# Routed experts: results scattered to (choice, token) rows, and read back by plain loads

## What is computed

```python
logits = xt @ Wr + br
probs = jax.nn.softmax(logits, axis=-1)
top_p, top_idx = jax.lax.top_k(probs, 2)            # two choices per token
weights = top_p / top_p.sum(axis=-1, keepdims=True)
h = gelu(xe @ W1 + b1)                              # per expert; hidden 256 in L0, 1024 in L1
y = h @ W2 + b2
out = (weights[:, :, None] * sel).sum(axis=1)       # sel: the two chosen experts' rows of y
x = x + out
```

## Time and profile before

| | us |
|---|---|
| median of 3 runs (5113.29 to 5120.27) | 5113.97 |
| the profiled execution, its own time | 5105.49 |
| span of that execution | 5103.5 |
| mean granted TensorE clock, share of full | 0.919 |
| L0: from the last `y` to the next phase's first instruction | 95.2 |
| L1: from the last `y` to the next phase's first instruction | 95.1 |

### The profile page before, as it was taken

The page is one execution under the profiler, slowest core; times in us unless marked ns, Lnnn a source line. Parts: engine busy times, 40 slices in busy tenths (PEclk is TensorE's granted clock), DMA queues, the critical chain, the costliest instruction groups (busy, mean ns, idle before and its releaser), DMA issues. The chain is left out here.

```text
span 5103.5 us, 70265 instructions
## 1 busy us (share of the span) xinstructions
PE 4142.4 (81%) x21605; PEld 3192.0 (63%) x21605; DVE 2765.3 (54%) x5823; ACT 1344.4 (26%) x2721; POOL 1845.0 (36%) x1628
## 2 busy tenths in 40 slices
PE   5899984664563999989999476998699999979978
PEld 2566652443552666658888465887587767758855
DVE  4588888887426999936666452001533322233354
ACT  0233330001223333322222032443100333420023
POOL 0477764554345676725666611111200000000011
PEclk9899997997686999989999777999799999989989
DMA  2599985540464666658777827997553100025300
GB/s 68 184 295 294 291 253 157 162 135 16 134 211 154 179 182 182 182 193 251 239 249 247 249 85 239 322 324 234 171 153 107 38 1 1 1 96 162 120 14 26
DMA packets 519630, 842.05 MB, mean 165 GB/s; under 512 B 80109, under 2 KB 365298, under 8 KB 519160
## 3 DMA queue, kind: packets, MB, share of 16 engines
q1 hardware_dynamic: 405810, 585.02, 35.9%
q0 software_dynamic: 62656, 189.33, 13.3%
q10 hardware_dynamic: 50820, 63.31, 3.6%
HBM read 567.81 MB, written 269.66 MB: 164 GB/s over the span
## 5 line engine op out<-in xcount | busy, mean ns | idle before, releaser
L2796 PE MATMUL sum_ps<-table_rows,block_weights 128*125 128x256 f32 x2500 | 563.2, 385 | 42.9 <-DMA table_rows<-k_table 42.8
L2796 PEld LDWEIGHTS sum_ps<-table_rows,block_weights 128*125 128x125 f32 x2500 | 463.4, 188 | 142.6 <-issue 75.6
L2610 POOL TENSOR_TENSOR running_blocks<-running_blocks,brought_blocks 128x650 f32<-128x650 f32 x320 | 439.1, 1372 | 254.9 <-DMA blocks<-running_blocks 236.9
L107 POOL DMA_INDIRECT rows_all<-kv_table,src_of_visit x416 | 439.0, 1055 | 221.4 <-issue 110.6
L2505 POOL DMA_INDIRECT gathered_rows<-k_table,src_of_chunk x392 | 407.3, 1039 | 207.7 <-issue 112.5
L2711 PE MATMUL sum_ps<-gathered_rows,hit 128*126 x1376 | 363.8, 390 | 23.4 <-DVE window_sums L2677 18.1
L2778 DVE TENSOR_TENSOR block_weights<-raw 128x625 f32<-128x625 f32 x248 | 184.6, 805 | 351.5 <-PE sum_ps L2796 322.5
L2041 DVE TENSOR_TENSOR y<-out_ps,b 128x256 f32<-128x256 f32 x120 | 50.9, 424 | 549.1 <-PE out_ps L1940 549.1
L2554 PE MATMUL block_ps<-cell_hot,low_hot 128*128 128x325 bf16 x1280 | 231.7, 304 | 139.8 <-DVE cell_hot L2544 139.2
L3288 POOL MEMSET eps<- 125x1 f32 x1 | 0.1, 98 | 917.0 <-POOLq L2738 917.0
L1104 PE MATMUL ps_sum<-summand,hit 128*125 128x261 f32 x832 | 211.6, 397 | 147.5 <-DVE odd_sums L1064 123.7
(11 more groups left out here) (494 smaller groups left out, 7931.6 us busy)
## 6 DMA issues: line engine op xcount, KB each, us to landing
w<-in_L_ffn_W SPq DMA_DIRECT2D x112, 1024.0 KB, 7.5
blocks<-running_blocks SPq DMA_DIRECT2D x320, 325.0 KB, 4.1
raw<-blocks SPq DMA_DIRECT2D x250, 325.0 KB, 3.5
v_kept<-rows_all SPq DMA_DIRECT2D x104, 512.0 KB, 5.1
v_rows<-v_kept SPq DMA_DIRECT2D x104, 512.0 KB, 3.6
visit_blocks<-block_copies ACTq DMA_DIRECT2D x320, 162.5 KB, 2.9
brought_blocks<-visit_blocks SPq DMA_DIRECT2D x320, 162.5 KB
w<-in_L_ffn_w SPq DMA_DIRECT2D x64, 256.0 KB, 3.5
```

What stands on the lines that cost most here:

```text
L107: pool.indirect_dma_start(env.ring[:, k % KEPT_RING, i, :], None, env.kv_table, bass.IndirectOffsetOnAxis(env.src_of_visit[:, k * VB + i:k ...
L2610: pool.tensor_tensor(self.sums[:, k % self.SUMS, :], self.sums[:, (k - 1) % self.SUMS, :], self.brought[:, k % self.BROUGHT, :], ALU.add). ...
L2796: mm = pe.matmul(sum_ps[0:P, t % banks, 0:D], weights[0:k, t % floats, h, :], rows[0:k, h, :], start=h == 0, stop=h == BH - 1)
```

## The change

Each slot gets a second number, `env.row_of_slot`: the row of (choice, token) in a new table `y_of_choice`, in which choice 0 takes the rows from 0 and choice 1 those from 4000 (APART = 32 tiles of 125); unused slots get rows of their own behind row 8000. The list is made in `Route.vector` by the same matmuls: the tile number put into `id_hot` now carries the choice (1 + 32 c + tile), and DVE takes it apart in 12 instructions where 2 stood.

In the experts' phase POOL writes a unit's `y` by indirect DMAs, one for each tile of 128 slots, to its rows of `y_of_choice`. These scatters of unit j - 4 stand behind the gathers of unit j in POOL's queue. SP's stores of `y` are gone. In the tail, SP waits until all scatters have landed and loads each token tile's two results by one plain DMA (125 partitions, two pieces of 1 KB each): eight at once, then five ahead of each group's stores in its queue. POOL's 50 gathers of the tail are gone, and the phase no longer reads `env.slots`.

```diff
+APART = 32
+SECOND = APART * P
+UNUSED = 2 * SECOND
...
-        done(v.tensor_copy(self.tile[:], env.iota[0:P, 0:T]))
+        for c in range(2):
+            done(v.tensor_scalar(self.tile[:, c, :], env.iota[0:P, 0:T], float(1 + c * APART), None, ALU.add))
...
         done(v.tensor_copy(self.row[:], row))
-        done(v.scalar_tensor_tensor(out=env.token_of_slot[:, 0:self.cut.parts], in0=tile, scalar=float(P), in1=self.row[:], op0=ALU.mult,
-                                    op1=ALU.add))
+        done(v.tensor_copy(self.slot_tile[:], tile))
+        done(v.scalar_tensor_tensor(out=self.row[:], in0=self.slot_tile[:], scalar=float(P), in1=self.row[:], op0=ALU.mult, op1=ALU.add))
...
-                def store(j, s):
-                    sp.dma_start(env.y_slots[ds(j * cut.unit, cut.unit), :].rearrange("(c p) d -> p c d", p=128), y[:, s]).then_inc(stored[s], 16)
+                def load_choice(t):
+                    s = t % n_choice
+                    if t >= n_choice:
+                        sp.wait_ge(x_made, t - n_choice + 1)
+                    sp.dma_start(choice[0:P, s], env.y_of_choice[0:UNUSED, :].rearrange("(c t p) d -> t p c d", c=2, p=P)[t]).then_inc(
+                        choice_landed[s], 16)
...
                 for s in range(n_slots):
-                    sp.wait_ge(copied, (cut.units - n_slots + s) * cut.tiles + 2 * cut.tiles)
-                    store(cut.units - n_slots + s, s)
+                    sp.wait_ge(stored[s], stored_base + 16 * cut.tiles * (cut.units // n_slots))
+                for t in range(n_choice):
+                    load_choice(t)
...
                 for g in range(G):
+                    for t in range(n_choice + g * GT, min(T, n_choice + (g + 1) * GT)):
+                        load_choice(t)
...
+                def scatter(j):
+                    s = j % n_slots
+                    pool.wait_ge(copied, (j + 2) * cut.tiles)
+                    for c in range(cut.tiles):
+                        at = j * cut.tiles + c
+                        pool.indirect_dma_start(env.y_of_choice, bass.IndirectOffsetOnAxis(env.row_of_slot[:, at:at + 1], 0),
+                                                y[:, s, c, :], None).then_inc(stored[s], 16)
...
-                for t in range(T):
-                    if t >= n_choice:
-                        pool.wait_ge(x_made, t - n_choice + 1)
-                    for c in range(2):
-                        pool.indirect_dma_start(choice[:, t % n_choice, c, :], None, env.y_slots, bass.IndirectOffsetOnAxis(
-                            env.slots[:, c, t:t + 1], 0)).then_inc(env.gathered[t % n_choice], 16)
+                    if j >= n_slots:
+                        scatter(j - n_slots)
+                for j in range(cut.units - n_slots, cut.units):
+                    scatter(j)
```

More of the change, by code:

```diff
@@ L1134, in __init__ @@
         self.part_f = sb(env, st, "part_f", [P, 2, 2, T])
-        self.tile = sb(env, st, "tile", [P, T], BF16)
+        self.tile = sb(env, st, "tile", [P, 2, T], BF16)
+        self.slot_tile = sb(env, st, "slot_tile", [128, cut.parts])
+        self.unused = sb(env, st, "unused", [128, cut.parts])
         self.lo_made, self.id_made, self.placed = [ph.sem() for _ in range(3)]
@@ L1231, in vector @@
             v.tensor_scalar(self.id_hot[:, c, :, 0], self.hi_hot[:], env.part[0:P, :], None, ALU.mult).then_inc(self.id_made, 1)
-            done(v.tensor_tensor(self.id_hot[:, c, :, 1], self.hi_hot[:], self.tile[:].unsqueeze(2).to_broadcast([P, T, self.cut.parts]),
+            done(v.tensor_tensor(self.id_hot[:, c, :, 1], self.hi_hot[:], self.tile[:, c, :].unsqueeze(2).to_broadcast([P, T, self.cut.parts]),
                                  ALU.mult))
@@ L1237, in vector @@
         done(v.tensor_copy(self.row[:], row))
-        done(v.scalar_tensor_tensor(out=env.token_of_slot[:, 0:self.cut.parts], in0=tile, scalar=float(P), in1=self.row[:], op0=ALU.mult,
-                                    op1=ALU.add))
+        done(v.tensor_copy(self.slot_tile[:], tile))
+        done(v.scalar_tensor_tensor(out=self.row[:], in0=self.slot_tile[:], scalar=float(P), in1=self.row[:], op0=ALU.mult, op1=ALU.add))
+        done(v.tensor_scalar(self.row[:], self.row[:], float(-P), None, ALU.add))
+        done(v.tensor_scalar(self.unused[:], self.slot_tile[:], float(APART), float(-SECOND), ALU.is_gt, ALU.mult))
+        done(v.tensor_tensor(self.unused[:], self.unused[:], self.row[:], ALU.add))
+        done(v.tensor_scalar(env.token_of_slot[:, 0:self.cut.parts], self.unused[:], 0.0, None, ALU.max))
+        done(v.tensor_scalar(self.unused[:], env.iota[:, 0:self.cut.parts], 128.0, env.part[:], ALU.mult, ALU.add))
+        done(v.tensor_scalar(self.unused[:], self.unused[:], float(UNUSED + P), None, ALU.add))
+        done(v.tensor_scalar(self.slot_tile[:], self.slot_tile[:], 1.0, None, ALU.is_lt))
+        done(v.tensor_tensor(self.unused[:], self.unused[:], self.slot_tile[:], ALU.mult))
+        done(v.tensor_tensor(env.row_of_slot[:, 0:self.cut.parts], self.unused[:], self.row[:], ALU.add))
 class TwoOfEight:
@@ L1825, in routed_experts_phase @@
         landed = [ph.sem() for _ in range(n_slots)]
-        stored = [ph.sem() for _ in range(n_slots)]
+        stored, stored_base = env.scattered, env.scattered_base
+        env.scattered_base += 16 * cut.tiles * (cut.units // n_slots)
         turned, x_ready, multiplied, activated, finished, copied = [ph.sem() for _ in range(6)]
@@ L1831, in routed_experts_phase @@
         first_gather = list(env.gathered_base)
-        first_choice = [b + 16 * cut.tiles * len(range(s, cut.units, n_slots)) * (s < n_slots) for s, b in enumerate(first_gather)]
-        for s in range(n_choice):
-            env.gathered_base[s] = first_choice[s] + 32 * len(range(s, T, n_choice))
+        for s in range(n_slots):
+            env.gathered_base[s] += 16 * cut.tiles * len(range(s, cut.units, n_slots))
+        choice_landed = [ph.sem() for _ in range(n_choice)]
         parts = [(w1, f"{kind}_ffn_{'w' if kind == 'L0' else 'W'}1"), (w2, f"{kind}_ffn_{'w' if kind == 'L0' else 'W'}2")]
@@ L1852, in load_weights @@
                     sp.dma_start(b2[:, s], a[f"{kind}_ffn_b2"][ds(e, 1), :].to_broadcast([128, D])).then_inc(landed[s], 16)
-                def store(j, s):
-                    sp.dma_start(env.y_slots[ds(j * cut.unit, cut.unit), :].rearrange("(c p) d -> p c d", p=128), y[:, s]).then_inc(stored[s], 16)
-                for s in range(n_slots):
-                    sp.sem_inc(stored[s], 1)
+                def load_choice(t):
[4 more added lines that the diff above has]
+                        choice_landed[s], 16)
                 for s in range(n_slots):
@@ L1868, in _ @@
                         load_weights(j + n_slots, s)
-                        store(j, s)
                 for s in range(n_slots):
-                    sp.wait_ge(copied, (cut.units - n_slots + s) * cut.tiles + 2 * cut.tiles)
-                    store(cut.units - n_slots + s, s)
+                    sp.wait_ge(stored[s], stored_base + 16 * cut.tiles * (cut.units // n_slots))
+                for t in range(n_choice):
+                    load_choice(t)
                 def rows_of(table, g):
@@ L2036, in copy_out @@
                 def copy_out(j, s, lap):
-                    v.wait_ge(stored[s], lap * 16 + 1)
+                    if lap > 0:
+                        v.wait_ge(stored[s], stored_base + 16 * cut.tiles * lap)
                     v.wait_ge(landed[s], lap * (16 * loads) + 16 * loads)
@@ L2057, in combine @@
                         s = t % n_choice
-                        v.wait_ge(env.gathered[s], first_choice[s] + 32 * (t // n_choice + 1))
+                        v.wait_ge(choice_landed[s], 16 * (t // n_choice + 1))
                         for c, made in enumerate((first_added, x_made)):
@@ L3564, in routing_buffers @@
     env.token_of_slot = sb(env, st, "token_of_slot", [128, max(c.parts for c in CUTS.values())], I32)
+    env.row_of_slot = sb(env, st, "row_of_slot", [128, max(c.parts for c in CUTS.values())], I32)
 def build(nc, a, out):
@@ L3573, in build @@
         env.gathered_base = [0] * RING
+        env.scattered = [st.enter_context(nc.semaphore(f"scattered_{s}")) for s in range(SLOTS)]
+        env.scattered_base = 0
         env.mean = sb(env, st, "mean", [P, T])
@@ L3596, in build @@
         env.token_table = nc.dram_tensor("token_table", (N, D), F32).ap()
-        env.y_slots = nc.dram_tensor("y_slots", (max(c.rows for c in CUTS.values()), D), F32).ap()
+        env.y_of_choice = nc.dram_tensor("y_of_choice", (UNUSED + max(c.rows for c in CUTS.values()), D), F32).ap()
         x_stack = ExitStack()
```

2 lines of the change are left out of this document (removed).

## The result

| | before | after |
|---|---|---|
| median of 5 runs, us | 5113.97 | 5165.11 |
| the profiled execution, its own time | 5105.49 | 5165.11 |
| mean granted TensorE clock | 0.919 | 0.914 |

The ratio is 1.0096, 95% interval 1.0073 to 1.0118: some 49 us slower, between 37 and 60. The forecast was +38, its range +14 to +66.

The account below looks back on a forecast made before the run. The prediction took PE to bound the loops and SP's stores to end L0's tail. Its terms, 5.4 + 13.2 + 18.9 + 0.5 = 38.0 us, on 5114 gave 5152 us, range 5128 to 5180.

Parts of the forecast that it names:

- What bounds the kernel: Both experts' phases before the change: PE bounds the loops, 4.29 us a unit in L0; SP's stores end L0's tail.
- The route list: Route lists of L0 and L1: 12 DVE instructions where 2 stood, about 2.7 us each, +5.4 us together.
- L0's loop: Loop of L0's experts' phase: four indirect DMAs a unit, 5.0 us against PE's 4.29, make POOL the bound; +13.2 us.
- I take 1.25: L0's loop: a scatter priced at 1.25 us, like a gather of the same count of rows.
- PE's clock as no term: L0's loop: PE busy some 85%, so no clock cost; an earlier stage busy 2.0 of 4.0 us had 1.00 granted.
- L0's hand-off: Between L0's loop and tail: SP may issue the first load 4.1 us after the last `y`.
- L0's tail: After L0's last `y`: loads and stores share a third of the DMA engines, 114.1 us against 95.2, +18.9.
- L1: Second experts' phase: its loop has slack on POOL and costs nothing; the tail's last load just fits, +0.5 us.
- Rival 1: L0's tail: loads don't queue with stores; -6, 5108 us, chance 0.12; with cheap scatters too -19, 5095, chance 0.05.
- Rival 2: L0's loop: scatters priced differently; free +25, 5139 us, chance 0.08; at 1.7 us each +62, 5176, chance 0.10.
- Rival 3: L1's loop: scatter traffic tips the DMA engines, 0.98 busy, over their limit; about +14 us, 5166, chance 0.05.
- Rival 4: Whole change: it doesn't do what it says; no size or chance of its own given.

## Why the prediction was right, point by point

The direction, the place and both mechanisms held; 46 us are found in the changed stretches where the forecast had 38.

- **What bounds the kernel**: right. PE's 4.29 us of a unit set L0's loop (with three indirect DMAs for each unit it is still 148.0 us), the stores its tail (spreading them alone took 10 us off).
- **The route list**: forecast +5.4, measured 4.9 behind the matmuls and 0.4 ahead of them, 5.3 in all.
- **L0's loop**: forecast +13.2, measured +18.1. What was mis-sized is one term, "I take 1.25": from a row of gathers that stood by themselves. Alternating with scatters an indirect DMA begins every 1.289 us, which over 107 steps is 4.2 us more. The first scatter came 16.28 us after the phase's first instruction where 15.1 was forecast: 0.9 because the first gathers landed 1.2 later, and 0.3 from `y` to the scatter, which the forecast left out. That landing is no effect of the scatters: from the phase's first instruction to the first turn it is 6.1 to 7.6 us in the kernels without scatters in L0. The last gather's 4.38 us to its turn (forecast 4.5) and PE's order behind it were right. The forecast's own terms add up to 12.9 (1499.7 less 1486.74), not 13.2. The bounds (0 to 37) held it with room.
- **PE's clock as no term**: what was carried over from the earlier trace rows failed, and the term came out small rather than nothing. The mean grant in the loop is 0.93, against 0.97 in the earlier trace rows. Behind a wait of 2.24 us for `rows` it fell from 1.00 (1496 to 1499) to 0.64 (1500 to 1502), and eight matmuls of `out_ps` took 2.91 us instead of 1.99 (1499.85 and 1505.72 above). POOL's steps didn't change by it, but the last two turns did: they come without a wait, so PE's slower stretch had a part in the end. The last turn lies 4.38 us behind the last gather; in the second run of the changed kernel, where it waited for `rows`, it lay 3.85 behind. So the clock cost some 0.5 us here, an estimate from these two distances.
- **L0's hand-off**: forecast 4.1 us, measured 1516.74 to 1520.81, 4.07. The match is partly luck: 0.29 from `y` to the first scatter was left out, and the landing took 2.51 from the last scatter's start instead of 2.8.
- **L0's tail**: forecast 110 us from the first issue, measured 112.6. The nearest reading, loads and stores on one third of the engines, was right. The rate was a little high: not 123 GB/s but 114 for loads alone (combines 2.24 us apart where 2.08 was forecast) and 119 to 121 with stores. The dry stretch was foreseen: 4 us at 0.12 where full is 0.33 are 2.5 us.
- **L1**: forecast +0.5, measured +1.8. "It just fits" was the weak step: the first combines are 2.16 us apart where 2.08 was forecast, and tiles 18, 19, 23 and 24 wait 0.75 to 1.28 us for their loads.
- **Rival 1** was to decide below 82 us from the first issue; it stood at 112.6, and fell. Its own price was also too low: with loads of 128 and stores of 125 the tail was 92.8, not 75.1, because later loads stand behind slow stores and behind the waits for their rows. It took both spread to reach 75.9.
- **Rival 2**, another price: slightly dearer, 0.04 us each. **Rival 3**: L1's loop went to a share of 0.99 and grew by 0.7 us, no more. **Rival 4**: no sign.

## What to carry to other kernels

Count the instructions that an engine must issue in one round of a loop and compare with the round of the engine that bounds it: the same scatter cost nothing at three indirect DMAs in 4.29 us and 18 us at four. Before replacing gathers by plain loads, look at the share of the DMA engines that a transfer of that exact partition count reaches in the trace; cut 125 into 120 and 5. And add the stretches that the change touches, not two whole profiles: the rest moved here by 13 us on its own.

## What the runs showed of the hardware

- The rate of loads alone fell from 275 GB/s at 128 partitions to 114 at 125 and 22.9 at 127; cut into 120 and 5 partitions, the 125 reached 243. A second queue (ACT's beside SP's) added nothing: five to seven packets were under way nearly all the time with one queue and with two.
- Indirect DMAs on POOL begin every 1.25 us when gathers follow each other and every 1.289 when gathers and scatters alternate. The idle time between them stays at 0.30; the instructions themselves are longer, 0.96 to 1.01 us instead of 0.95. Why isn't settled.
- One wait of 2.24 us, in a loop in which PE was otherwise busy, was followed by a granted clock of 0.57 over the next 4 us (1500 to 1504), a mean of the levels of 2.4 and 1.2 GHz, and by 1.00 again from 1504 on.
